# A decoder layer on one core: the state-space layer's skip term is written into PSUM by ScalarE, and TensorE's other products come in runs of four

## The reference

```python
xr = x @ W_in.T
xc, res = (xr[..., :DI], xr[..., DI:])                 # DI = 1024 channels
u = silu(causal_conv4(xc) + b_conv)
x_dbl = einsum('bdl,ed->ble', u, W_xproj)              # dt (32), B (16), C (16)
delta = softplus(dt @ W_dt.T + b_dt)
h = exp(delta * A) * h + delta * B * u                 # 16 states, along the 512 steps
y = (h * C).sum(states) + u * D                        # u * D is the skip term
x = layernorm(x + (y * silu(res)) @ W_out.T)
```

## Time and profile before

| | |
|---|---|
| time, median of 3 runs | 2580.58 us (2575.85 to 2581.28) |
| the profiled execution | 2579.53 us, its span 2577.7 us |
| main loop of the state-space part, pass 4 | 205.3 us (686.0 to 891.3) |
| second part of the kernel (attention, feed-forward) | from about 1743 us to the end |

### The profile page before, as it was taken

One profiled execution on the slowest core, in us unless ns is written; L12 is line 12 of the kernel. 1 busy time (PEld: TensorE's weight loads), 2 busy tenths in 40 slices (PEclk: granted clock), 3 DMA queues, 4 the chain that ended last, 5 costly groups with the idle time before them and its releaser, 6 DMA issues. The chain is left out here.

```text
span 2577.7 us, 38451 instructions
## 1 busy us (share of the span) xinstructions
PE 2409.9 (93%) x15488; PEld 1426.6 (55%) x15488; DVE 1822.4 (71%) x2154; ACT 1475.5 (57%) x2258; POOL 1668.7 (65%) x912
## 2 busy tenths in 40 slices
PE   6899999999999999999999989877999999999997
PEld 3466566656566666656656666544445554554543
DVE  2898798798798799789889879841465355456443
ACT  2587577677678678667757867631333443333332
POOL 0698899888899889879988989951333134133130
PEclk8899999999999999999999999988999999999998
DMA  3777978977978987897897797755000010000000
GB/s 125 202 162 161 239 162 173 245 162 167 234 164 180 207 196 165 177 232 156 179 238 156 166 223 151 168 107 202 1 17 17 33 33 1 33 33 1 17 17 17
DMA packets 158832, 342.75 MB, mean 133 GB/s; under 512 B 39232, under 2 KB 102208, under 8 KB 127808
## 3 DMA queue, kind: packets, MB, share of 16 engines
q0 software_dynamic: 27648, 201.34, 39.7%
q1 hardware_dynamic: 131008, 138.97, 16.4%
HBM read 119.57 MB, written 19.37 MB: 54 GB/s over the span
## 5 line engine op out<-in xcount | busy, mean ns | idle before, releaser
L898 POOL TENSOR_TENSOR mamba_ring<-mamba_ring,mamba_c_row 128x1024 f32<-128x1024 f32 x512 | 1277.0, 2627 | 66.4 <-DVE mamba_ring L789 65.0
L789 DVE TENSOR_TENSOR_SCAN mamba_ring<-mamba_ring,ps 128x512 f32<-128x512 f32 x1024 | 1180.5, 1203 | 188.6 <-PE ps L381 187.7
L635 ACT ACTIVATE mamba_ring<-mamba_delta,mamba_a_neg 128x512 f32<-128x512 f32 x1024 | 661.1, 711 | 102.9 <-DMA mamba_ring<-mamba_ring 101.7
L381 PEld LDWEIGHTS ps<-mamba_diag_b,mamba_v_t 64*128 64x128 f32 x8192 | 503.2, 189 | 321.9 <-issue 244.2
L381 PE MATMUL ps<-mamba_diag_b,mamba_v_t 64*128 64x128 f32 x8192 | 594.2, 285 | 34.6 <-DVE mamba_ring L789 33.8
L296 PE MATMUL ps<-mamba_xt,mamba_wu 128*128 128x512 f32 x512 | 254.9, 626 | 33.8 <-DMA mamba_wu<-w_u 16.9
L907 POOL DMA_DIRECT2D mamba_ring<-mamba_ring x192 | 179.4, 934 | 139.6 <-DMA mamba_ring<-mamba_ring 102.3
L349 PE MATMUL ps<-mamba_xt,mamba_wres 128*128 128x512 f32 x512 | 256.6, 619 | 0.0
L1552 POOL TENSOR_TENSOR xf_pr<-xf_pr,xf_top 128x1232 f32<-128x1232 f32 x32 | 75.0, 2343 | 275.7 <-DVE xf_top L1470 275.7
L402 PE MATMUL ps<-mamba_ident,mamba_ring 128*128 128x128 f32 x1024 | 145.9, 289 | 40.4 <-DMA mamba_ring<-mamba_ring 40.4
L1545 POOL TENSOR_TENSOR xf_xn<-xf_xn,xf_bo_s 128x512 f32<-128x512 f32 x32 | 39.5, 1267 | 222.2 <-PE xf_ps L1122 222.2
(11 more groups left out here) (116 smaller groups left out, 2904.1 us busy)
## 6 DMA issues: line engine op xcount, KB each, us to landing
mamba_ring<-mamba_ring POOLq DMA_DIRECT2D x192, 1024.0 KB, 7.8
mamba_c_row<-c_rows SPq DMA_DIRECT2D x32, 1024.0 KB, 15.5
mamba_wu<-w_u SPq DMA_DIRECT2D x64, 256.0 KB, 3.3
mamba_wres<-w_res SPq DMA_DIRECT2D x64, 256.0 KB, 6.1
mamba_diag_b<-b_diagonals SPq DMA_DIRECT2D x56, 256.0 KB, 14.2
mamba_xt<-x_t SPq DMA_DIRECT2D x8, 1024.0 KB, 15.8
mamba_xres<-x SPq DMA_DIRECT2D x32, 256.0 KB, 8.3
x<-mamba_xres SPq DMA_DIRECT2D x32, 256.0 KB, 5.1
```

The lines of the kernel that those rows point to most:

```text
L381: m = nc.tensor.matmul(ps[:, 2 * s + i, tb * P:(tb + 1) * P], v_t[g % 2][i * H:(i + 1) * H, tb * P:(tb + 1) * P], diag_b[i * H:(i + 1) * H ...
L635: a = nc.scalar.activation(ring[:, q % NR, i, :], delta[:, d % EARLY, :], ACT.Exp, scale=a_neg[:, d, 2 * k + i:2 * k + i + 1])
L789: m = nc.vector.tensor_tensor_scan(ring[:, r, i, :], ring[:, r, i, :], both[:, bass.ds(i, T, 2)], 0.0, ALU.mult, ALU.add)
L898: nc.gpsimd.tensor_tensor(ring[:, q % NR], ring[:, q % NR], c_row[:, 2 * k:2 * k + 2, :], ALU.mult).then_inc(c_done, 1)
```

## The change

ScalarE now does `take_yt` first and then writes u D straight into the PSUM bank of y, with time along the free axis (`scale_skip`, now in step 7). `y_transposes` no longer overwrites the bank but accumulates onto it (start=False), and waits for both. `skip_transposes` is gone. TensorE's work of 512 columns is gathered: `u_product` is called with all four calls in steps 1 and 5, `res_product` with all four in step 3 (step 5 in block 6), `x_product` with four in steps 1 and 5, and the output projection in runs of 2 to 5 calls in steps 1, 3, 5 and 7. Some additions on VectorE move by one or two steps with them.

```diff
-            def skip_transposes(g):
+            def y_transposes(g):
+                pe.wait_ge(yt_ready, g + 1)
                 pe.wait_ge(du_ready, g + 1)
                 for tb in range(TT):
-                    nc.tensor.matmul(ps[:, y_bank(g), tb * P:(tb + 1) * P], y_t[:, tb * P:(tb + 1) * P], ident[:],
-                                     is_transpose=True, start=False, stop=False, skip_group_check=True)
-
-            def y_transposes(g):
-                pe.wait_ge(yt_ready, g + 1)
-                for tb in range(TT):
-                    m = nc.tensor.transpose(ps[:, y_bank(g), tb * P:(tb + 1) * P], y_t[:, tb * P:(tb + 1) * P],
-                                            ident[:])
+                    m = nc.tensor.matmul(ps[:, y_bank(g), tb * P:(tb + 1) * P], y_t[:, tb * P:(tb + 1) * P], ident[:],
+                                         is_transpose=True, start=False, stop=(tb == TT - 1), skip_group_check=True)
                 m.then_inc(y_back, 1)
...
                 if k == 6 and g >= 1:
-                    state_sum(g - 1, SUMS[0])
-                    skip_transposes(g - 1)
-                    state_sum(g - 1, SUMS[1])
+                    for e in SUMS:
+                        state_sum(g - 1, e)
                 if k == 4 and g + 1 < NG:
                     v_transposes(g + 1)
                 if feeds and d < 5:
                     n = (b + 1) * ND + FIRST_U[d]
-                    if k < 2:
-                        u_product(n, BANK_A, [2 * k, 2 * k + 1])
-                    if k in (4, 5) and d in TWO_U:
-                        u_product(n + 1, BANK_A, [2 * k - 8, 2 * k - 7])
+                    if k == 1:
+                        u_product(n, BANK_A, range(KT))
+                    if k == 5 and d in TWO_U:
+                        u_product(n + 1, BANK_A, range(KT))
                 if feeds and d == 5:
-                    if k in (0, 1):
-                        x_product(b + 1, [2 * k, 2 * k + 1])
-                    if k in (4, 5):
-                        x_product(b + 1, [2 * k - 4, 2 * k - 3])
+                    if k in (1, 5):
+                        x_product(b + 1, range(k - 1, k + 3))
...
-                if d in (0, 4):
-                    if k == 3:
-                        res_product(g, [0, 1])
-                    if k == 7:
-                        res_product(g, [2, 3])
-                if d in (1, 5, 7):
-                    if k == 2:
-                        res_product(g, [0, 1])
-                    if k == 3:
-                        res_product(g, [2, 3])
-                if d in (2, 3):
-                    if k == 3:
-                        res_product(g, [0, 1])
-                    if k == 4:
-                        res_product(g, [2])
-                    if k == 7:
-                        res_product(g, [3])
-                if d == 6:
-                    if k == 5:
-                        res_product(g, [0, 1])
-                    if k == 7:
-                        res_product(g, [2, 3])
+                if k == (5 if d == 6 else 3):
+                    res_product(g, range(KT))
...
                 if d == 6:
-                    if k == 0:
-                        out_first(b, 0, [2, 3])
                     if k == 1:
-                        out_first(b, 1, [0, 1])
-                    if k == 2:
-                        out_first(b, 1, [2])
+                        out_first(b, 0, [2, 3, 4])
                     if k == 3:
-                        out_first(b, 0, [4])
-                        out_first(b, 1, [3])
-                    if k == 4:
-                        out_first(b, 1, [4])
+                        out_first(b, 1, [0, 1, 2, 3, 4])
+                    if k == 7:
+                        out_first(b, 2, [0, 1])
                 if d == 7:
-                    if k == 0:
-                        out_first(b, 2, [0, 1])
                     if k == 1:
-                        out_first(b, 2, [2, 3])
-                    if k == 4:
-                        out_first(b, 2, [4, 5])
+                        out_first(b, 2, [2, 3, 4, 5])
                     if k == 5:
-                        out_first(b, 3, [0, 1])
+                        out_first(b, 3, [0, 1, 2, 3])
                     if k == 7:
-                        out_first(b, 3, [2, 3, 4])
+                        out_first(b, 3, [4])
...
-                if back and (d, k) == (3, 2):
+                if back and (d, k) == (3, 0):
...
             def scale_skip(g):
                 b, d = g // ND, g % ND
+                act.wait_ge(yt_ready, g + 1)
+                nc.scalar.activation(ps[:, y_bank(g), :], u[b % 2][:, d, :], ACT.Copy,
+                                     scale=dsk[:, d:d + 1]).then_inc(du_ready, 1)
+
+            def take_yt(g):
+                act.wait_ge(summed, (g + 1) * NSUM)
                 if g >= 1:
                     act.wait_ge(y_back, g)
-                nc.scalar.activation(y_t[:], u[b % 2][:, d, :], ACT.Copy,
-                                     scale=dsk[:, d:d + 1]).then_inc(du_ready, 1)
-
-            def take_yt(g):
-                act.wait_ge(summed, (g + 1) * NSUM)
                 nc.scalar.copy(y_t[:], ps[:, y_bank(g), :]).then_inc(yt_ready, 1)
...
-                if k == 2 and g >= 1:
-                    scale_skip(g - 1)
                 if k == 7 and g >= 1:
                     take_yt(g - 1)
+                    scale_skip(g - 1)
...
-                if back and (d, k) == (3, 3):
+                if back and (d, k) == (3, 1):
...
-                if (d, k) == (6, 4):
+                if (d, k) == (6, 3):
                     add_first(b, 0)
                 if (d, k) == (6, 5):
                     add_first(b, 1)
-                if (d, k) == (7, 5):
+                if (d, k) == (7, 3):
                     add_first(b, 2)
```

More of the change, by code:

```diff
@@ L533, in step @@
                     dt_pair(b, 2)
-                if back and (d, k) == (1, 6):
+                if back and (d, k) == (1, 7):
                     pe.wait_ge(vt_ready, g + 2)
-                    out_second(b - 1, 0, y_bank(g), [5])
-                if back and (d, k) == (1, 7):
-                    out_second(b - 1, 0, y_bank(g), [6, 7])
+                    out_second(b - 1, 0, y_bank(g), [5, 6, 7])
                 if back and (d, k) == (2, 5):
@@ L574, in _ @@
                         step(b, d, k)
-            state_sum(NG - 1, SUMS[0])
-            skip_transposes(NG - 1)
-            state_sum(NG - 1, SUMS[1])
+            for k in SUMS:
+                state_sum(NG - 1, k)
             y_transposes(NG - 1)
@@ L646, in scale_skip @@
                 b, d = g // ND, g % ND
-                if g >= 1:
-                    act.wait_ge(y_back, g)
-                nc.scalar.activation(y_t[:], u[b % 2][:, d, :], ACT.Copy,
+                act.wait_ge(yt_ready, g + 1)
+                nc.scalar.activation(ps[:, y_bank(g), :], u[b % 2][:, d, :], ACT.Copy,
                                      scale=dsk[:, d:d + 1]).then_inc(du_ready, 1)
@@ L653, in take_yt @@
                 act.wait_ge(summed, (g + 1) * NSUM)
+                if g >= 1:
+                    act.wait_ge(y_back, g)
                 nc.scalar.copy(y_t[:], ps[:, y_bank(g), :]).then_inc(yt_ready, 1)
@@ L748, in _ @@
                         step(b, d, k)
+            take_yt(NG - 1)
             scale_skip(NG - 1)
-            take_yt(NG - 1)
             for tb in range(0, TT, 2):
```

## The result

The changed kernel takes 2563.79 us (median of 4 runs, 2557.05 to 2566.44) against 2580.86 (2575.85 to 2581.28) for the kernel before: a ratio of 0.9938, 95% interval 0.9917 to 0.9958. It is faster, by 17 us of the median where 36 were forecast. The profiled execution took 2566.20 us, 13.3 less than that of before; its span is 2564.3.

What follows compares the result with a forecast made beforehand. TensorE was taken as the bound. Work of 191.4 us plus 8.1 of waits made a middle pass 199.5 against 205.3; six passes gave 35 us, 36 with the ends, so 2545 us, range 2518 to 2579.

Steps and rivals of the forecast that it cites:

- TensorE's work: Middle pass: skip transposes gone and 11 fewer stretches at 0.30 us; 198.4 to 191.4 us, 7.0 a pass, 55 in all.
- The sum for a middle pass: TensorE's work 191.4 us plus waits of 8.1 gives 199.5 against 205.3, a gain of 5.8 a pass.
- x of the next pass: Step 0 of block 0: the 2.0 us wait for x counted as gone, the product moving about 2.1 us later.
- The y transposes lose their cover: Blocks 0, 2, 3 and 4, step 7: TensorE waits 0.3 to 0.9 us for ScalarE, four times a pass.
- Longer runs, later results: Later last taps delay VectorE: block 4 slower by 1.3 us, waits in blocks 4, 0, 1 of 2.0, 1.3, 0.2.
- Merge wait: TensorE's wait for the last merge's DMA in a middle pass: 2.3 us, unchanged.
- the allowance of 1.0 for GpSimd and DMA: Part of a middle pass's waits: 1.0 us for GpSimd and DMA being nearly full.
- Six passes like this one: The middle pass's gain of 5.8 us taken for six passes: 35 us.
- First and last pass: First pass not bound by TensorE, last has few stretches to lose: half a microsecond gained in each.
- GpSimd and DMA take over: Rival: merges land later, GpSimd's waits grow by 3 to 4 us a pass; gain 15 to 20, 2562 us; chance 0.13.
- Slower: the last taps: Rival: 56 u products end late, 1.2 us each on the path costs 67 us; at 1.6, 2603 us; chance 0.13.
- Nothing is left: Rival: only the skip's 28 us come; VectorE's lag and y waits take them; within 5 us of 2580; chance 0.08.

Runs made afterwards that it cites:

- x_earlier: Changed kernel with block 7's gate projection in step 1 and its output projection in step 3, so x's load is issued earlier: 2567.61 us.
- thin pair: Kernel before and changed kernel, each with merges adding only one of the two ring slots: 2525.68 and 2506.53 us.
- u_halves: Changed kernel with the input projection again in two pieces of two calls (steps 0 and 1, 4 and 5): 2573.46 us.
- y_later: Changed kernel with the y transposes moved from step 7 to behind the batch of step 0 of the next block: 2575.47 us.
- gate_in_7: Changed kernel with the gate projection of blocks 0, 2, 3 and 4 in step 7, ahead of the y transposes: 2619.67 us.
- after_no_skip: Changed kernel with the skip term left out (no write by ScalarE, y transposes wait for the copy only): 2572.96 us.

## Why the prediction was wrong

The direction, TensorE's work and block 4 were right; the size was twice what came. The step that failed is **The sum for a middle pass**: it set TensorE's waits at 8.1 us a pass, 1.5 more than before. They rose by 4.6 on the mean of the six middle passes: 2.5 for the skip write, 1.3 for merges, 1.0 for scans, 0.3 less for x. So a middle pass gave 2.85 us, not 5.8. And the sum took the ends of the kernel as half a microsecond to the good each, where they cost nearly 4 us. The terms one by one, for the fourth pass where no other is named:

- *TensorE's work* (0.30 us per stretch, 0.43 for skip transposes, 7.0 per pass): right, 191.45 us against 191.4; 54.2 us in all against 55. A run of four starts the next batch after 3.63 us (687.09 to 690.72).
- *x of the next pass*, counted as gone: wrong, 1.8 us stayed. The product that waits moved back 2.1 us, but x's load waits for the last gate projection of block 7, and with four calls in a run this ends 1.7 us later than before. Demand and supply moved by nearly the same amount. An earlier issue does not cure it (x_earlier took 2 us off the waits in all); without the loads of B and C beside it x is in time in all passes but one.
- *The y transposes lose their cover*, 0.3 to 0.9 us four times: right in kind, measured 0.82, 0.40, 0.40 and 1.23 (one above the range; the sum had counted only two of the four, as the wait for VectorE was to swallow the others). The skip write took 691 ns, 17 less than the same activation into SBUF. That bears out in direction what the Trainium skill says (ScalarE: Activation LUTs, Step-by-step: what each stage is for), that PSUM is ScalarE's nearer destination; the size is nearly nothing here.
- *Longer runs, later results*: right for block 4 (25.23 against 25.3) and for the wait of taps (10.6 us a pass, forecast 6 to 10). Of the 3.3 us for blocks 4 and 0, 2.6 came (1.23 + 0.53 and 0.82, most of it as the wait for ScalarE). **Wrong for the two blocks that were not walked**: block 1 has 1.11 us of scan wait (forecast 0.2), block 3 and its end 0.68 + 1.06 (forecast 0.3). Blocks 5 to 7 together became 2.9 us shorter, as forecast.
- *Merge wait* 2.2, as forecast 2.3; the allowance of 1.0 for GpSimd and DMA wasn't needed in this pass, but in the mean pass, where merge waits rose from 2.1 to 3.4 us. Sum: 8.1 + 1.8 (x) + 0.9 + 1.4 (blocks 1 and 3) - 0.7 (blocks 0 and 4) - 1.0 - 0.3 (rest) = 10.2, as measured.
- *Six passes like this one*: from one pass's first scan to the next's, the six middle passes took 202.3, 208.4, 205.3, 205.9, 206.9 and 207.5 us before, mean 206.05, and 201.6, 202.5, 201.8, 204.0, 207.4 and 201.9 after, mean 203.2. So the gain is 2.85 a pass, where the fourth alone has 3.5 and the forecast 5.8. The difference of 0.65 lies in the merges: these waits fell by 0.1 us in the fourth pass and rose by 1.3 on the mean of six.
- *First and last pass*, half a microsecond each to the good: wrong. The first went from 205.0 to 206.1 us. From the last one's first scan to the last VectorE instruction of the state-space part it went from 225.7 to 230.0, with TensorE's wait for the very last merge 3.2 longer (10.9 to 14.1). The second part was 1.7 shorter. In the first, TensorE isn't the bound, as I wrote; that its later results cost without a gain there is argued, not shown. 36 - 14 (sum of a pass) - 4 (other passes) - 5 (ends: 4 lost and 1 forecast) = 13, against 13.3 of the profiled executions.
- *The rivals.* "GpSimd and DMA take over" gave 2562 us and the time is 2564, but it was right mostly by luck: its sign was GpSimd's waits for merges 3 to 4 us per pass longer; they rose from 98.1 to 118.7 us over 1600, 2.6 per pass, and the thin pair shows that more than half of TensorE's saving is lost without them. Merges took a part, 7.9 us of TensorE's time in the six passes. "Slower: the last taps" had the right mechanism at a quarter of its price (in u_halves the earlier last taps take 48.6 - 29.9 = 18.7 us off the scan waits, not 67). The price of "Nothing is left" was loosely added: 1.3 to 2.0 twice and 0.5 four times over six passes give 28 to 36 us, not 28.

What stays open: what a repair of either wait would bring. In each of three attempts (y_later, gate_in_7, after_no_skip) waits for scans rose when the wait for ScalarE went, which would fit a chain through VectorE that can only be relieved as a whole. But the first two made y late for VectorE by their own edit, and in the third and in y_later TensorE's waits did not grow in sum, only its busy time. An edit that brings the skip write forward without delaying y was not tried.

## What to carry to other kernels

TensorE was 97% busy in the pass, but in some blocks the chain from batch to scan to freed bank was as long as its own work (in block 4 after the change, 25.2 us against 23.3 in my walk). Work taken off a bound engine gives time only up to the next chain, so walk every block of the pass, not the one that looks worst, and add the waits that remain. When work is gathered into long runs, the last result of a run is late by the run's length: price who waits for it, and for a load, what frees its buffer. When an experiment moves work, look at who waits for its result too: y_later and gate_in_7 held up VectorE by 30 and 42 us. And check the tool of an experiment: halving a DMA's bytes by columns made it dearer to issue.

## What the runs showed of the hardware

A merge's issue on GpSimd took 935 ns with 27,648 packets over the kernel and some 1,570 to 1,730 with 101,376 packets of half the bytes in all; with one slot, again 27,648 packets, 986. The median from issue to landing was 7.8 us for 1 MB before and 5.0 for 0.5 MB in the thin pair. The Trainium skill (DMA: Bandwidth & Descriptors, Anatomy of one DMA — SWDGE (gpsimd) path) gives 2.0 us plus the bytes at 436 GB/s, an estimate of 4.4 and 3.2 us. Both measured values are above it, with the DMA engines 82% and 54% busy.

The wait below cost more than itself. In u_halves, TensorE in order of time at the end of a pass:

```profile
1287.15 1.16 PE L381 MATMUL ps<-mamba_diag_b,mamba_v_t 64*128 64x128 f32 x16
1293.64 3.64 PE L402 MATMUL ps<-mamba_ident,mamba_ring 128*128 128x128 f32 x16 [5.32 <-DMA mamba_ring<-mamba_ring]
1297.21 1.16 PE L381 MATMUL ps<-mamba_diag_b,mamba_v_t 64*128 64x128 f32 x16
```

The stages view of that stretch of u_halves:

```profile
1285.00:1300.00 15.00, 9.68 (x62) 6.90 (x62) 5.42 (x6) 6.80 (x12) 10.76 (x7) 0.77 1.03 238
```

After 5.32 us without work the granted clock of these 15 us is 0.77, so part of them ran at the 1.2 GHz level, and 16 transposes take 3.57 us to the next start instead of 1.90 (780.28 to 782.18 in the changed kernel). DMA is full there (1.03), as the next pass's loads meet the merge.

The clock moves whole passes too. Before the change, the 1505 matmul records of a middle pass take 198.6 to 198.8 us in passes 2, 4 and 5, with a granted clock of 1.00, and 201.7 to 202.1 in passes 3, 6 and 7, with 0.98. So a pass moves by some 3 us without any change in its work, as much as the change brings it.
